# Macaron block on one core: swap order, score bank for the values, and rotation sums on GpSimd

## The reference

```python
x = x + 0.5 * ffn(layernorm(x))
x = x + attn(layernorm(x))
x = x + 0.5 * ffn(layernorm(x))          # the same weights
```

```python
q, k, v = (einsum('bsd,dnh->bsnh', x, w) for w in (wq, wk, wv))
r1 = x1 * cos - x2 * sin;  r2 = x2 * cos + x1 * sin      # of q and of k, pairs of columns
probs = softmax(where(causal, q k^T / sqrt(128), -1e30))
out = einsum('bqnh,nhd->bqd', probs v, wo)
```

## Time and profile before

| what | us |
|---|---|
| median of 3 runs (lowest to highest) | 1486.59 (1485.44 to 1487.28) |
| the profiled execution, its own time | 1487.64 |
| its span, first to last instruction | 1485.6 |
| busy: PE / weight load | 1413.1 / 1212.3 |
| busy: DVE / ACT / POOL | 1099.9 / 911.7 / 791.3 |
| mean granted clock of TensorE | 0.993 of full |

### The profile page before, as it was taken

One profiled execution on the slowest core, in us unless ns is written; L12 is line 12 of the kernel. 1 busy time (PEld: TensorE's weight loads), 2 busy tenths in 40 slices (PEclk: granted clock), 3 DMA queues, 4 the chain that ended last, 5 costly groups with the idle time before them and its releaser, 6 DMA issues.

```text
span 1485.6 us, 24040 instructions
## 1 busy us (share of the span) xinstructions
PE 1413.1 (95%) x8164; PEld 1212.3 (82%) x8164; DVE 1099.9 (74%) x2331; ACT 911.7 (61%) x1826; POOL 791.3 (53%) x694
## 2 busy tenths in 40 slices
PE   6999999689999999999999999999999989999998
PEld 4778888578888888888888888888888877878886
DVE  7776776877777777777777777777777787775665
ACT  4544444577767767777677767776777755544433
POOL 4655354365565556555655555556555643755443
PEclk9999999899999999999999999999999999999999
DMA  4000001000000000000000000000000020000000
GB/s 167 1 1 1 1 1 50 22 8 2 23 1 8 23 1 8 22 1 9 22 1 8 2 21 4 6 22 1 8 8 1 2 109 3 1 15 1 15 15 15
DMA packets 11415, 23.29 MB, mean 16 GB/s; under 512 B 928, under 2 KB 5024, under 8 KB 11168
## 3 DMA queue, kind: packets, MB, share of 16 engines
q1 hardware_dynamic: 11296, 21.78, 4.3%
HBM read 19.68 MB, written 2.10 MB: 15 GB/s over the span
## 4 chain that ended last, share of the span: by engine, by line
PE 59%; DVE 20%; ACT 10%; issue 8%; POOL 3%; DMA 0%; DVEq 0%; ACTq 0%; POOLq 0%
PE ps L1533 18%; PE ps L1535 17%; PE ps L1534 17%; PE ps L1927 5%; ACT before_h L929 3%; DVE ps L1411 3%; DVE rot L1377 3%; DVE own_l L344 3%; ACT swapped L906 3%; DVE before_l L344 2%; ACT swapped L905 2%; POOL um_l L344 1%; DVE v_l L344 1%; DVE hid L1157 1%; POOL hid_l L344 1%
## 5 line engine op out<-in xcount | busy, mean ns | idle before, releaser
L700 POOL TENSOR_SCALAR probs<-probs,inv_sum 128x128 f32<-128x128 f32 (+7 forms) x256 | 219.4, 857 | 321.7 <-DVE inv_sum L1396 321.7
L952 ACT ACTIVATE probs<-ps,neg_max 128x128 f32<-128x128 f32 (+7 forms) x256 | 190.2, 743 | 126.6 <-DVE neg_max L1411 126.5
L1411 DVE CUSTOM_DVE_ANT_0 ps<-ps,causal 128x128 f32<-128x128 f32 (+7 forms) x256 | 193.9, 757 | 93.2 <-PE ps L1535 93.1
L689 POOL TENSOR_TENSOR rot_sin<-swapped,rope 128x512 f32<-128x512 f32 x128 | 165.6, 1294 | 110.4 <-ACT swapped L906 110.4
L344 POOL TENSOR_TENSOR hid_l<-hid,hid_h 128x512 fp32r<-128x512 f32 x80 | 109.4, 1369 | 189.1 <-ACT hid_h L800 189.1
L1927 PE MATMUL ps<-ident,probs 128*128 128x128 f32 x1152 | 177.6, 277 | 25.0 <-DVE before_l L344 15.2
L1927 PEld LDWEIGHTS ps<-ident,probs 128*128 128x128 f32 x1152 | 132.8, 141 | 54.7 <-issue 21.2
L344 DVE TENSOR_TENSOR before_l<-ps,before_h 128x512 fp32r<-128x512 f32 x128 | 88.3, 690 | 101.8 <-ACT before_h L929 101.8
L1533 PE MATMUL ps<-k_h,q_h 128*128 128x384 f32 (+5 forms) x384 | 151.2, 394 | 0.7 <-issue 0.7
L344 DVE TENSOR_TENSOR own_l<-ps,own_h 128x128 fp32r<-128x128 f32 (+3 forms) x256 | 123.8, 484 | 10.6 <-ACT own_h L929 10.6
L1535 PE MATMUL ps<-k_h,q_l 128*128 128x384 f32 (+5 forms) x384 | 131.6, 343 | 0.0
(11 more groups left out here) (201 smaller groups left out, 4404.8 us busy)
## 6 DMA issues: line engine op xcount, KB each, us to landing
w_raw<-attn_w SPq DMA_DIRECT2D x32, 256.0 KB, 2.8
w_in<-ffn_w SPq DMA_DIRECT2D x12, 576.0 KB, 8.5
x_sb<-x_in SPq DMA_DIRECT2D x4, 512.0 KB, 5.6
out<-x_sb SPq DMA_DIRECT2D x3, 512.0 KB, 3.1
rope<-rope_w SPq DMA_DIRECT2D x1, 1024.0 KB, 6.8
w_in<-ffn_w SPq DMA_DIRECT2D x2, 264.0 KB, 4.1
expand_raw<-expand_w SPq DMA_DIRECT2D x2, 256.0 KB, 5.1
out<-x_sb SPq DMA_DIRECT2D x2, 256.0 KB, 2.1
```

What stands on the lines that cost most here:

```text
L689: pool.tensor_tensor(rot_sin[:], swapped[:], rope[:, 1, 512 * ch:512 * ch + 512], ALU.mult)\
L700: pool.tensor_scalar(probs[s % 4][:, 0:n], probs[s % 4][:, 0:n], inv_sum[:, s % 4:s % 4 + 1], 1.0, ALU.mult, ALU.mult).then_inc(probs_read ...
L952: act.activation(probs[t % 4][:, 0:a * n].rearrange("p (a n) -> p a n", a=a), view, ACT.Exp, bias=neg_max[:, t % 4:t % 4 + 1], scale=-1.0, ...
L1411: dve.tensor_tensor_reduce(out=view, in0=view, in1=causal[:, SEQ - a * n:].rearrange("p (a n) -> p a n", a=a), scale=-SCALE, scalar=HUGE, ...
```

## The change

- `MISC_BANKS`: the projection of step 0 goes into bank 7 (before: 1), and the values of step 7 into bank 1, a score bank (before: 7). PE waits there for the exponentials so far.
- The first projection of a unit is swapped by ACT in step 1, behind the copies of the transposed tile (before: at the end of step 0). POOL's sine product of it moves to step 1 too.
- `rope_sum` goes from DVE to POOL, right behind the sine product of the same rotation. On POOL the low part of the rotation before now stands ahead of the sine product.
- `LOW_FIRST_AT` has step 6 as well: one low part ahead of the maximum.
- The split of the values' weights moves from step 25 to 27.
- First pair: the scores of step 0 go ahead of the projection; the values no longer wait for x there; the last rows are transposed in step 1 into banks 6 and 1, their high parts are made in step 2 and their low parts in step 3; `value_low` of the first values moves to step 1 ahead of `rope_low_part`.
- Last pair: two output projections one step earlier and into bank 3, with statistics, normalisation and its transposes one step earlier.
- Second FFN: in `first_setup` the statistics and the aggregation stand later among the masks.

```diff
--- before.py
+++ after.py
@@ -82,8 +82,10 @@
 T_BANK, PV_BANK = 4, 6
 FIRST_PROJECTIONS = [U, S1, S0, D1]
 FIRST_VALUES = [D1, D2, S1]
-
-MISC_BANKS = [1, 3, 7, 3, 7, 7, 7, 7]
+LAST_ROWS_BANKS = (OUT0, G)
+
+MISC_BANKS = [7, 3, 7, 3, 7, 7, 7, 1]
+DRAIN_BANK = 7
 
 
 UNITS = 4
@@ -93,11 +95,11 @@
 T_LAG = 2
 ROPE_LAG = 2
 
-LOW_FIRST_AT = {1: 2, 2: 1, 7: 2}
+LOW_FIRST_AT = {1: 2, 2: 1, 6: 1, 7: 2}
 
 LATE_ROTATION_AT = 2
 
-PAIR_SPLITS_AT = {"o": 13, "v": 25, "k": 21, "q": 23}
+PAIR_SPLITS_AT = {"o": 13, "v": 27, "k": 21, "q": 23}
 DRAIN_STEPS = 9
 
 
@@ -108,18 +110,18 @@
 DRAIN_O_AT = {33: 0, 37: 1}
 
 Y_AT = {3: 0, 5: 1, 9: 2, 11: 3}
-LAST_Y_AT = [{19: 0, 21: 1, 25: 2, 27: 3}, {34: 0, 35: 1, 38: 2, 39: 3}]
-
-LAST_Y_BANKS = {25: 7, 27: 7, 34: 7, 35: 1, 38: 7, 39: 1}
-
-
-
-
-
-STATS_AT = [20, 22, 27, 28, 36, 37]
-AGGREGATE_AT = [22, 28, 37]
-NORM_AT = [(24, 25), (29, 30), (39, 39)]
-TURN_AT, TURNED_LOW_AT = [(26, 26), (31, 31)], [(27, 27), (32, 32)]
+LAST_Y_AT = [{18: 0, 19: 1, 25: 2, 27: 3}, {34: 0, 35: 1, 38: 2, 39: 3}]
+
+LAST_Y_BANKS = {18: 3, 19: 3, 25: 7, 27: 7, 34: 7, 35: 1, 38: 7, 39: 1}
+
+
+
+
+
+STATS_AT = [20, 21, 27, 28, 36, 37]
+AGGREGATE_AT = [21, 28, 37]
+NORM_AT = [(23, 24), (29, 30), (39, 39)]
+TURN_AT, TURNED_LOW_AT = [(25, 25), (31, 31)], [(26, 27), (32, 32)]
 SPLIT_AT = [27, 33, 35]
 LOGITS_AT, TURN_LOGITS_AT = (32, 33), 34
 PICK_AT, PEAK_AT, SHIFT_AT, SUM_AT, WEIGH_AT = 35, 36, 36, 37, 38
@@ -471,7 +473,7 @@
 
         def misc_bank(t):
 
-            return MISC_BANKS[t % SEQ_TILES] if t < STEPS else MISC_BANKS[-1]
+            return MISC_BANKS[t % SEQ_TILES] if t < STEPS else DRAIN_BANK
 
         def rotation_to_end(p, t, first, last):
 
@@ -689,6 +691,11 @@
                 pool.tensor_tensor(rot_sin[:], swapped[:], rope[:, 1, 512 * ch:512 * ch + 512], ALU.mult)\
                     .then_inc(proj_sin, 1)
 
+            def rope_sum(index, k):
+                pool.wait_ge(proj_cos, index + 1)
+                pool.wait_ge(proj_sin, index + 1)
+                pool.tensor_tensor(rot[:, k % 2], rot[:, k % 2], rot_sin[:], ALU.add).then_inc(proj_rot, 1)
+
             def attention(p, first, last):
                 for t in range(STEPS + (DRAIN_STEPS if last else 0)):
                     q, s = tile_at(p, t - 1)
@@ -699,12 +706,15 @@
                         pool.nop(nofuse=True)
                         pool.tensor_scalar(probs[s % 4][:, 0:n], probs[s % 4][:, 0:n], inv_sum[:, s % 4:s % 4 + 1], 1.0,
                                            ALU.mult, ALU.mult).then_inc(probs_ready, 1)
-                    side = side_work(p, t, first, last)
-                    if side and side[0] == "proj":
-                        rope_sin(side[2], side[3] // 2)
                     turn = rotation_to_end(p, t, first, last)
                     if turn:
                         rope_low_part(pool, turn[2], turn[1], turn[3])
+
+                    behind = 1 if t % SEQ_TILES == 1 else 0
+                    side = side_work(p, t - behind, first, last) if t % SEQ_TILES != 0 else None
+                    if side and side[0] == "proj":
+                        rope_sin(side[2], side[3] // 2)
+                        rope_sum(side[2], side[3])
                     if last:
 
                         for c, at in enumerate(AGGREGATE_AT):
@@ -929,6 +939,9 @@
                         act.activation(turned_place(i, n, True),
                                        ps[:, bank, 0:P * count].rearrange("p (a b) -> p a b", a=count),
                                        ACT.Copy).then_inc(pT_high, 1)
+                    before = side_work(p, t - 1, first, last) if t % SEQ_TILES == 1 else None
+                    if before and before[0] == "proj":
+                        swap_halves(before[2], misc_bank(t - 1))
                     turn = rotation_to_end(p, t, first, last)
                     if turn and t % SEQ_TILES != LATE_ROTATION_AT:
                         rope_high(turn[2], turn[1], turn[3])
@@ -959,9 +972,9 @@
                         value_high(2, 0, 2, FIRST_VALUES[2])
                     if first and t == 1:
                         rope_high(3, 0, 3)
-                    if first and t == 0:
-                        layer_norm_high(2 * CHUNKS - 1, CHUNKS - 1)
-                    if side and side[0] == "proj":
+                    if first and t == 2:
+                        layer_norm_high(2 * CHUNKS - 1, CHUNKS - 1, LAST_ROWS_BANKS)
+                    if side and side[0] == "proj" and t % SEQ_TILES != 0:
                         swap_halves(side[2], misc_bank(t))
                     for kind, at in PAIR_SPLITS_AT.items():
                         if t == at and (kind == "o" or not last):
@@ -1229,12 +1242,15 @@
                 mask_low_rank(g, UM_UP)
                 mask_low_rank(g, UM_UP_STEP)
                 um_first_low(g, UM_UP)
-                if f == 1:
+                mask_low_rank(g, UM_GATE)
+                if f == 0:
+                    mask_low_rank(g, UM_GATE_STEP)
+                    um_first_low(g, UM_GATE)
+                else:
                     stats_pair(2 * CHUNKS - 1)
+                    um_first_low(g, UM_GATE)
+                    mask_low_rank(g, UM_GATE_STEP)
                     aggregate(last, 1)
-                mask_low_rank(g, UM_GATE)
-                mask_low_rank(g, UM_GATE_STEP)
-                um_first_low(g, UM_GATE)
 
             def ffn_chunk(f, c):
                 g = CHUNKS * f + c
@@ -1472,9 +1488,6 @@
                         invert_sum(p, t, first)
                     for group in groups[:ahead]:
                         turned_low(*group)
-                    turn = rotation_to_end(p, t, first, last)
-                    if turn and t % SEQ_TILES != LATE_ROTATION_AT:
-                        rope_sum(turn[2], turn[3])
                     if t % SEQ_TILES == 0:
                         invert_sum(p, t, first)
                     if t < STEPS and not (first and t == 0):
@@ -1483,15 +1496,12 @@
 
                         if t == 1:
                             rope_sum(3, 3)
+                            value_low(0, 0, 0, FIRST_VALUES[0])
                         rope_low_part(dve, 2 + t, 0, 2 + t)
-                    if first and t == 0:
-                        layer_norm_low(2 * CHUNKS - 1, CHUNKS - 1)
                     for group in groups[ahead:]:
                         turned_low(*group)
-                    if turn and t % SEQ_TILES == LATE_ROTATION_AT:
-                        rope_sum(turn[2], turn[3])
                     side = side_work(p, t, first, last)
-                    if first and 1 <= t < 4:
+                    if first and 2 <= t < 4:
                         value_low(t - 1, 0, t - 1, FIRST_VALUES[t - 1])
                     if side and side[0] == "proj":
                         rope_cos(side[2], side[3], misc_bank(t))
@@ -1504,6 +1514,8 @@
                         low(dve, o_place(u, c, False), ps[:, PV_BANK, :], o_place(u, c, True)).then_inc(o_ready, 1)
                     if t % 2 == 0 and t % SEQ_TILES != 0:
                         invert_sum(p, t, first)
+                    if first and t == 3:
+                        layer_norm_low(2 * CHUNKS - 1, CHUNKS - 1, LAST_ROWS_BANKS)
                     for kind, at in PAIR_SPLITS_AT.items():
                         if t == at + 1 and (kind == "o" or not last):
                             split_pair(kind, p + (kind != "o"))
@@ -1592,8 +1604,8 @@
                 if bank in bank_user:
                     kind, index = bank_user[bank]
                     pe.wait_ge({"proj": proj_swapped, "v": v_ready, "o": y_added, "norm": xnT_ready}[kind], index + 1)
-                elif bank == MISC_BANKS[-1]:
-                    pe.wait_ge(xnT_ready, KT * 2 * CHUNKS)
+                elif bank == OUT1:
+                    pe.wait_ge(x_updated, 2 * CHUNKS)
 
             def norm_to_turn(c, kt):
 
@@ -1890,6 +1902,9 @@
                 else:
                     if t >= STEPS - SEQ_TILES and k == 0:
                         pe.wait_ge(wa_ready["v"], p + 2)
+                    if misc_bank(t) == 1:
+
+                        pe.wait_ge(exp_done, STEPS * p + t)
                     values(index, what, k, misc_bank(t))
 
             def scores(p, t, first):
@@ -1970,19 +1985,17 @@
 
             def attention(p, first, last):
                 for t in range(STEPS + (DRAIN_STEPS if last else 0)):
+                    if t < STEPS:
+                        scores(p, t, first)
+                    side(p, t, first, last)
                     if first and t == 0:
-                        side(p, t, first, last)
-                        scores(p, t, first)
 
                         pe.wait_ge(wa_ready["v"], 1)
-                        pe.wait_ge(x_updated, 2 * CHUNKS)
                         for k, bank in enumerate(FIRST_VALUES):
                             values(k, 0, k, bank)
-                        layer_norm(2 * CHUNKS - 1, xn_last)
-                    else:
```

(6 more changed lines are left out.)

## The result

The changed kernel takes 1479.08 us (1477.29 to 1479.76, 5 runs) where the kernel before takes 1487.28 beside it: a ratio of 0.9947, 95% interval 0.9935 to 0.9958. It is 0.5% faster. I forecast 1471 and 1.1%; the sign was right and the time lies in the range, the size was off by half.

A forecast was written before the change was run, and what follows sets the result against it. PE, busy 1413.1 of 1485.6 us, bounds the kernel, its waits set by ACT's order. Gains 4.2 + 8.8 + 0 + 1.3 + 0 + 0 + 1.5 = 15.8 off 1487.64 give 1471.8, as run median 1471 us; range 1461 to 1483.

The forecast's parts named there:

- The late swap, units 1 and 3, and the split: Swap moved to step 1, split to 27: unit 1 gains 0.53 in 8 units (4.2), unit 3 1.26 in 7 (8.8).
- units 0 and 2: Late swap there: the 0.5 saved at step 1's transposes is lost one step later; gain 0, bounds -0.2 and +0.5 each.
- the walk met PE to 0.0: Unit 1, chain behind the late swap: it ends at 670.72, when PE also arrives, so nothing is lost at step 2's weighing.
- Rival A: The wait only moves, to step 2's weighing in units 1 and 3 too: 7.7 gained, 1479 us; chance 0.14.
- Bank and low part: Values' bank at step 7, low part first at step 6: 0.08 gained in 23 units, 0.07 lost in 8; 1.3.
- the additions: Rotation sums moved from DVE to GpSimd, 128 at 1.29 against 0.69: hidden by GpSimd's slack, worth 0.
- The new wait at step 7: PE at tile 5's transposes waits for `before_l`, behind ACT's exponential and swap: 0.53 of stall becomes 0.45.
- rival C: GpSimd becomes late and PE waits 1.0 in each of 31 units: 15 slower, 1502 us; chance 0.10.
- the collision of two instructions: GpSimd and two-SBUF-input DVE instructions exclude each other; without it tile 2's scaling shrinks from 1.03 to some 0.6.
- Start: First pair: steps 0 to 2 come 2 to 4 us earlier, later waits offset it; 0, bounds -2 and +2.
- The wait for the bank: First pair, step 4: scores wait for bank G until `layer_norm_low` ends at 289.5, against 289.19 before.
- End: Last pair gains 2.0 at the weighing and step 28, second FFN's transposes lose 0.5: 1.5, bounds 0 and 3.

The follow-up runs named there:

- e5: Kernel before with the first projection's swap and its GpSimd sine product moved to step 1, and the values' weight split at step 27: 1481.47 us.
- e2: Kernel before with only the first projection's swap and its GpSimd sine product moved to step 1: 1482.03 us.
- e14: Changed kernel with every unit's first-projection swap back at the end of step 0, its sine product and addition in step 0: 1480.54 us.
- e1: Kernel before with only the split of the values' weights moved from step 25 to 27: 1483.60 us.
- e6: Changed kernel with the rotation's additions back on DVE and no low part ahead of the maximum in step 6: 1477.97 us.
- e8: Changed kernel with step 6's swap behind step 7's copies, its sine product and addition on GpSimd in step 7: 1456.31 us.
- e9: Changed kernel with step 6's swap behind step 7's copies, and step 0's swap delayed only in units 1 and 3, behind o's copy: 1450.85 us.
- e11: Changed kernel with the second FFN's first-chunk statistics and aggregation ahead of the gate's masks again: 1477.70 us.
- e12: Changed kernel with the last pair's output projections, statistics, normalisation and its transposes at their earlier kernel's steps: 1480.70 us.
- e10: e9 with the rotation's additions back on DVE and no low part ahead of the maximum in step 6: 1467.01 us.

## Why the prediction was right in sign and wrong in size

**The late swap, units 1 and 3, and the split: 4.2 + 8.8 = 13.0 forecast, 6.7 measured** (0.83 in eight pairs, e5; 5.7 by the run times). This is the step that failed, in three places. In units 0 and 2, which I had put at zero with -0.2 as a bound, the late swap costs 0.27 alone (e2) and 0.36 inside the changed kernel (e14), in each of 16 units. The walk had the copy of values 7.01 into the unit (1174.42 in one that starts at 1167.41); it starts at 7.20 (635.27 - 628.07), behind two tile copies, the swap and the copy of o in a row without a pause, and every low part behind it comes later by as much. In unit 1 the walk met PE to 0.0 and the trace shows 0.17 lost at the weighing; of the 0.53 forecast 0.29 came (e2). In unit 3 it was 1.09 of 1.26 (e5); there I also had both waits fall by the split's move, and e1 shows that the split held only the second one. Rival A, the wait only moves, was thus true for nearly half in unit 1, for an eighth in unit 3, and more than wholly in the even units. And the whole late swap, undone in the changed kernel (e14), turned out to be worth 0.03 a pair: what odd units gain by it even ones lose.

**Bank and low part, 1.3, and the additions, 0: together 1.8 measured** (0.22 in eight pairs, e5 to the changed kernel). Since e6, with the additions on DVE and no low part first, lasts as long as the changed kernel, neither of them gives this 0.22; what e6 and e5 still differ by in the middle pairs is the banks and GpSimd's order. That the sum of 1.3 and 0 came near the 1.8 is luck in so far as the low part, in my 1.3, gives nothing. The new wait at step 7 was forecast as 0.45 and is 0.57, 0.75 in unit 1, where the o split stands in step 13. I named its cause, ACT's exponential and swap, and left it at that, though moving that swap too was worth another 22.8 us (e8).

**GpSimd.** Its additions hold 1.29, as forecast (124 of them and not 128, since the first four stay on DVE):

```profile
L691 POOL TENSOR_TENSOR rot_sin<-swapped,rope x128: 1267/1287/1745, 257.7 to 1187.3; 128x512 f32<-128x512 f32 x128
L697 POOL TENSOR_TENSOR rot<-rot,rot_sin x124: 1263/1288/1548, 282.5 to 1188.7; 128x512 f32<-128x512 f32 x124
```

The tightest scaling, of tile 2 (against the earlier trace rows):

```profile
644.10 0.59 POOL L707 TENSOR_SCALAR probs<-probs,inv_sum 128x384 f32<-128x384 f32 x1
```
```profile
646.18 0.49 PE L1942 MATMUL ps<-ident,probs 128*128 128x128 f32 x3
```

has 1.49 of slack, where I had 1.1; rival C was far off. GpSimd pays 1.29 for what DVE does in 0.69. In the changed kernel itself that bought nothing (e6); in e9's order it is worth 16 us, together with the low part that goes first. The Trainium skill's rule (GPSIMD Engine Reference, 3.1 Elementwise) gives the price of the operation and says nothing of the path.

The scaling of tile 2 fell from 1.03 to 0.59, the number I had forecast from the collision of two instructions. The traces show that collision. In the kernel before, the addition on DVE begins 0.14 behind GpSimd's `k_l` (646.29, 1.29 long) and takes 1.69, to 0.54 behind the end of `k_l`; the scaling begins under it and takes 1.03. In e6, where DVE makes the additions as well but GpSimd has its new order, the scaling begins 0.13 ahead of the addition and keeps its 0.60, and the addition takes 1.00. DVE and GpSimd before, then in e6:

```profile
646.43 1.69 DVE L1383 TENSOR_TENSOR rot<-rot,rot_sin 128x512 f32<-128x512 f32 x1 [0.26 <-POOL rot_sin L689]
647.56 1.03 POOL L700 TENSOR_SCALAR probs<-probs,inv_sum 128x384 f32<-128x384 f32 x1
```
```profile
644.50 1.00 DVE L1398 TENSOR_TENSOR rot<-rot,rot_sin 128x512 f32<-128x512 f32 x1 [0.83 <-POOL rot_sin L691]
644.37 0.60 POOL L707 TENSOR_SCALAR probs<-probs,inv_sum 128x384 f32<-128x384 f32 x1
```

The first is so for 31 of the 32 scalings of this size before (the one that meets no addition takes 0.59), the second for 30 of 32 in e6; in the changed kernel none meets an addition. So the one that starts second is the one that becomes longer. That agrees with the lock of which the Trainium skill speaks (SBUF — State Buffer, SBUF: two separate sides). My cause was thus right for the changed kernel, where no addition is left to meet; what I missed is that GpSimd's new order, which starts the scaling first, is enough by itself: all scalings together take 219.4 us before, 197.7 in the changed kernel, and 198.9 in e6.

**Start: 0 forecast.** The first pair gained 1.75 to the second pair's start, and its share of the swap, split and bank accounts for about 1. What is left, 0.7, is less than the 2.3 by which e11 and e12, the same up to there, differ; so the runs neither confirm nor refute the 0. The scores of step 4 and the transposes of step 6 (against the earlier trace rows) stand at my 289.5 and 300.2:

```profile
289.39 0.61 PE L1545 MATMUL ps<-k_h,q_h 128*128 128x320 f32 x1 [3.62 <-issue]
...
300.30 0.77 PE L1942 MATMUL ps<-ident,probs 128*128 128x128 f32 x5 [1.43 <-POOL probs L707]
```

The wait for the bank is the one I had described, and it is 3.62 in e11 and e12 as well; but the scores stand at 290.91 and 287.97 there, so that agreement to 0.1 is luck.

**End: 1.5 forecast, 0.2 measured** from the last pair's start. Its parts were 2.0 and -0.5 and measure 2.3 and -1.0 (e12, e11). Of the 1.1 between that sum and the 0.2, 0.6 stands in the last unit: its transposes of steps 5 to 7 wait 0.36, 1.09 and 0.33 before and 0.65 and 1.78 in the changed kernel, and e12 has the last two as well, so that they don't come from the last pair's order. I had no term for it. The rest stays open; kernels that have the same last part differ by 0.6 in that stretch (377.3 before, 377.9 in e1). The weighing that was 1.65 late no longer waits. The wait for the bank at step 28 is gone, and the wait for the second FFN's spread is the one that grew (against the earlier trace rows):

```profile
1251.52 1.94 PE L1558 MATMUL ps<-ident,spread 128*128 128x128 f32 x8 [3.65 <-DVE spread L1044]
```

What stays open besides: which of the banks and GpSimd's order gives the 0.22 a pair (neither was undone alone), and the two parts of e10's 16 us beyond what the places tell.

## What to carry to other kernels

When one engine copies for three others, the order in its queue is the resource, and each copy whose consumer is far away belongs behind the copy whose consumer is the bound engine; look at every step where they meet and not only at the one with the largest wait. When a walk ends with "the chain meets PE to 0.0", it has not shown that nothing is lost: an error of 0.2 in one start is all of the result, times the units. Edits that relieve an engine off the path are worth what the order lets through: the same additions were worth 0 in one order and, with the low part that they make room for, 16 us in the next. Last, a forecast that comes out right within the spread of two executions of one kernel has not been tested.

## What the runs showed of the hardware

**The clock around the first pair** differs between executions whose instructions are the same up to there. The windows 270 to 280 and 280 to 290 us of the changed kernel, then of e11 (columns: window, length, busy time and count of PE, PEld, DVE, ACT, POOL, granted clock, DMA share, GB/s):

```profile
270.00:280.00 10.00, 8.81 (x60) 7.81 (x59) 9.12 (x24) 5.07 (x11) 3.95 (x4) 0.95 0.24 79
280.00:290.00 10.00, 3.53 (x14) 2.53 (x15) 6.66 (x17) 6.97 (x17) 8.34 (x8) 0.91 0.00 1
```
```profile
270.00:280.00 10.00, 8.91 (x43) 8.15 (x43) 8.78 (x22) 4.32 (x9) 3.90 (x3) 0.60 0.26 79
280.00:290.00 10.00, 5.28 (x32) 3.93 (x30) 6.37 (x18) 7.48 (x17) 6.30 (x7) 0.91 0.00 1
```

The granted clock of the first window is 0.95 in the one and 0.60 in the other. In both PE had just waited 1.94 for DVE, until 267.35 and 267.41, and from 268 to 270 both stand at 0.50, the lower of the two levels (1.2 GHz); the changed kernel is back at 1.00 (2.4 GHz) from 272 on, e11 is still at 0.50 from 276 to 278. The second unit starts at 304.74 and 305.86. The first scores start between 268.3 and 270.3 in the 13 kernels with the changed kernel's first pair, and between 270.1 and 272.3 in the 4 with that of before, where a projection stands ahead of them. A difference of 2 us between two spans can be that alone, which is why the pairs are compared here.

**Two engines, one of which waits inside its instruction.** A DVE addition with both inputs in SBUF and a GpSimd scaling that overlap show no idle time; the one that starts second is longer, 1.03 instead of 0.59 for the scaling, 1.00 and, across two GpSimd instructions, 1.69 instead of 0.69 for the addition. A duration above the median of its kind is the sign to look for in a trace.
